# Two walks over sorted edges: a tile-wise ring of 44 instead of two chunk buffers of 20 tiles, and half the descriptor scratch

## The reference

```python
h = (x @ W).reshape(n, heads, out_ch)
al_s = einsum('nhc,hc->nh', h, a_src); al_d = einsum('nhc,hc->nh', h, a_dst)
logits = leaky_relu(al_s[src] + al_d[dst], 0.2)
m = segment_max(logits, dst)                 # per target node
e = exp(logits - m[dst]); denom = segment_sum(e, dst)
out = segment_sum(h[src] * (e / denom[dst]), dst)
```

## Time and profile before

| | us |
|---|---|
| median of 3 runs | 6598.26 |
| lowest and highest | 6596.5 and 6599.07 |
| profiled execution, its own time | 6614.21 |
| profiled execution, span of the core | 6612.5 |
| first walk, in the profile | about 200 to 2850 |
| second walk | about 2850 to 5700 |

### The profile page before, as it was taken

How to read it: one execution, slowest core, us unless ns; L and a number is a source line. 1 busy time by engine, 2 the same in 40 slices (tenths; PEclk the granted TensorE clock), 3 DMA queues, 4 the chain that set the end, 5 groups by cost and what they waited for, 6 DMA issues and landing times. The chain is left out here.

```text
span 6612.5 us, 83222 instructions
## 1 busy us (share of the span) xinstructions
PE 4639.7 (70%) x21069; PEld 3502.2 (53%) x21069; DVE 3115.5 (47%) x8587; ACT 2833.9 (43%) x8419; POOL 3628.4 (55%) x3778
## 2 busy tenths in 40 slices
PE   7477777777777777773556565665555555699999
PEld 4355555555555555552344444444443434588887
DVE  4355656655566656662444444444444444711111
ACT  2455655655556555673434334343232223322222
POOL 0556665665566656535666666666666664234443
PEclk9788898888889888996777777676677777699999
DMA  5667777777777767733444444444455554453332
GB/s 194 191 194 199 203 201 195 200 201 198 197 197 203 202 191 198 197 106 108 117 118 115 119 115 116 120 114 116 117 135 140 138 138 115 155 188 129 128 132 78
DMA packets 703586, 1027.53 MB, mean 155 GB/s; under 512 B 391738, under 2 KB 483736, under 8 KB 702862
## 3 DMA queue, kind: packets, MB, share of 16 engines
q0 software_dynamic: 229312, 718.64, 38.9%
q1 hardware_dynamic: 473246, 302.52, 15.8%
q10 hardware_dynamic: 560, 1.05, 0.1%
HBM read 951.81 MB, written 65.48 MB: 154 GB/s over the span
## 5 line engine op out<-in xcount | busy, mean ns | idle before, releaser
L861 POOL DMA_INDIRECT walk_ring<-s_h,walk_index x3320 | 3167.7, 954 | 2138.2 <-issue 1018.1
L1022 PE MATMUL walk_pM<-walk_ring,walk_hit 128*128 128x262 f32 (+1 forms) x9960 | 3013.1, 454 | 233.6 <-issue 138.8
L1022 PEld LDWEIGHTS walk_pM<-walk_ring,walk_hit 128*128 128x128 f32 x9960 | 2140.1, 224 | 788.1 <-issue 377.3
L886 ACT ACTIVATE walk_ring<-walk_ring 128x128 f32<-128x128 f32 (+1 forms) x6640 | 2138.8, 414 | 19.1 <-issue 13.0
L1252 DVE TENSOR_TENSOR acc<-walk_pM,acc 128x520 f32 (+1 forms) x1494 | 832.5, 557 | 1789.4 <-remote 997.3
L876 ACT ACTIVATE walk_ring<-walk_gap 128x40 f32<-128x40 f32 (+1 forms) x249 | 54.0, 258 | 2582.1 <-DVE walk_gap L1214 2020.0
L926 PE MATMUL walk_pC<-all_ident,walk_best 128*84 128x128 f32 (+1 forms) x166 | 57.4, 346 | 904.5 <-DVE walk_best L1170 639.2
L1219 DVE TENSOR_TENSOR walk_hit<-walk_pK,walk_meta 128x512 f32<-128x512 f32 x830 | 560.2, 675 | 11.8
L926 PEld LDWEIGHTS walk_pC<-all_ident,walk_best 128*84 128x84 f32 (+1 forms) x166 | 19.7, 119 | 970.2 <-issue 970.0
L2061 ACT ACTIVATE expert_hT<-expert_pH,expert_b 128x256 f32<-128x256 f32 x448 | 187.8, 470 | 601.1 <-PE expert_pH L2113 601.0
L2113 PE MATMUL expert_pH<-expert_xT,expert_w 128*128 128x256 f32 x1792 | 398.9, 381 | 6.7 <-DVE expert_xT L2071 5.9
(11 more groups left out here) (314 smaller groups left out, 4245.3 us busy)
## 6 DMA issues: line engine op xcount, KB each, us to landing
walk_hitT<-s_places SPq DMA_DIRECT2D x166, 640.0 KB
expert_w<-in_fw_dram SPq DMA_DIRECT2D x64, 1024.0 KB, 12.0
walk_ring<-s_h,walk_index POOLq DMA_INDIRECT x3320
walk_goal<-walk_target SPq DMA_DIRECT2D x830, 6.0 KB
walk_goal<-walk_target SPq DMA_DIRECT2D x830, 1.5 KB
walk_xk<-s_xT SPq DMA_DIRECT2D x98, 128.0 KB
walk_resets<-s_resets SPq DMA_DIRECT2D x415, 20.0 KB
s_h<-first_h_out SPq DMA_DIRECT2D x7, 1056.0 KB, 4.3
```

Source lines behind the costliest of these rows:

```text
L861: pool.indirect_dma_start(ring[:, r % RS, t, :], None, table, bass.IndirectOffsetOnAxis(ap=index[:, r % TS, t:t + 1], axis=0)).then_inc(ro ...
L886: last = nc.scalar.activation(row, row, ACT.Copy, scale=ring[:, r % RS, t, at + FH:at + FH + 1])
L1022: last = nc.tensor.matmul(pM[:, b, a, 0:WIDE], hit[:, (r * CGROUPS + g) % HBUF, t % GROUP, :], ring[:, r % RS, t, a * HALF_ROW:a * HALF_RO ...
```

## The change

The ring becomes a ring of tiles: `[P, RT, A * HALF_ROW]` with RT = 44 tiles in the first walk (60 in the second, which is the same size as before). Tile t of chunk c lies at slot (c * 20 + t) mod RT. `AHEAD` becomes RT // TPS: 22 steps in the first walk and 30 in the second. Since 44 isn't a multiple of 20, some chunks of the first walk wrap round the end, and every operation on a whole chunk is done there in two pieces. The semaphores `rows_in` become 3 in both walks, the index buffers 5 instead of 6, and `TURN`, after which the written-out phases repeat, 30 instead of 6. Three small tiles share one, and the descriptor scratch is 8192 bytes.

```diff
-TURN = 6
+TURN = 30
...
-    RS = 2 if H > 1 else 3
-    TS = 6
+    RT = 44 if H > 1 else 60
+    TS = 5
...
-    AHEAD = RS * CS
+    AHEAD = RT // TPS
+    RS = 3
+    assert RT % GROUP == 0 and RT >= 2 * CT
...
-        ring = m.sb("ring", [P, RS, CT, A * HALF_ROW])
+        ring = m.sb("ring", [P, RT, A * HALF_ROW])
...
+        small = m.sb("small", [P, 8])
+        carry, reset0, ratio = small[0:RK, 0:2], small[0:1, 2:4], small[0:1, 4:4 + H]
...
+        def slot(c, t):
+
+            return (c * CT + t) % RT
+
+        def pieces(c):
+
+            head = min(CT, RT - slot(c, 0))
+            return [slice(0, head)] + ([slice(head, CT)] if head < CT else [])
...
-                            pool.indirect_dma_start(ring[:, r % RS, t, :], None, table,
+                            pool.indirect_dma_start(ring[:, slot(c, t), :], None, table,
...
                     for a in range(A):
-                        nc.scalar.activation(terms_of(r).rearrange("p (t a) h -> p t a h", a=A)[:, :, a, :],
-                                             gap[:, a * HP:(a + 1) * HP, 1:].rearrange("p h t -> p t h"), ACT.Exp)
+                        for tiles in pieces(n):
+                            nc.scalar.activation(terms_of(n, tiles).rearrange("p (t a) h -> p t a h", a=A)[:, :, a, :],
+                                                 gap[:, a * HP:(a + 1) * HP, 1:].rearrange("p h t -> p t h")[:, tiles, :], ACT.Exp)
...
+                    for tiles in pieces(n):
+                        own = terms_of(n, tiles).rearrange("p (t a) h -> p a h t", a=A)
+                        for a in range(A):
+                            heads = slice(a * HP, (a + 1) * HP)
+                            last = nc.vector.tensor_tensor(best[:, heads, 1 + tiles.start:1 + tiles.stop], own[:, a, :, :],
+                                                           dt[:, tiles, heads].rearrange("p t h -> p h t"), ALU.max)
                     last.then_inc(best_ready, 1)
...
+                    for tiles in pieces(n):
+                        for a in range(A):
+                            nc.vector.tensor_tensor(tail(n, tiles, HP * (FH + 1))[:, :, a, :],
+                                                    peak_h[:, a * HP:(a + 1) * HP, 1:].rearrange("p h t -> p t h")[:, tiles, :],
+                                                    spread(meta[:, r % IS, 1, tiles], 2, HP), ALU.mult)
...
-                        nc.vector.tensor_copy(weight_k, ring[:, r % RS, :, at])
+                        for tiles in pieces(n):
+                            nc.vector.tensor_copy(weight_k[:, tiles], slots_of(n, tiles)[:, :, at])
...
-    nc = bacc.Bacc("TRN2", target_bir_lowering=False, num_devices=1)
+    nc = bacc.Bacc("TRN2", target_bir_lowering=False, num_devices=1, dynamic_dma_scratch_size=8192)
```

More of the change, by code:

```diff
@@ L739, in tables_of, with slots_of, tail, terms_of @@
             return (i * (TURN // IS) + r // IS + 1) * 32
[L741 to L747, removed]
+        def slot(c, t):
[3 more added lines that the diff above has]
+            return [slice(0, head)] + ([slice(head, CT)] if head < CT else [])
+        def slots_of(c, tiles):
+            return ring[:, slot(c, tiles.start):slot(c, tiles.start) + tiles.stop - tiles.start, :]
+        def tail(c, tiles, lo):
+            return slots_of(c, tiles).rearrange("p t (a c) -> p t a c", a=A)[:, :, :, lo:lo + HP]
+        def terms_of(c, tiles):
+            return by_head(slots_of(c, tiles).rearrange("p t c -> p (t c)"), HP, FH)[:, :, :, FH]
         m.clear_semaphores()
@@ L884, in scale @@
                             at = h // HP * HALF_ROW + h % HP * (FH + 1)
-                            row = ring[:, r % RS, t, at:at + FH]
-                            last = nc.scalar.activation(row, row, ACT.Copy, scale=ring[:, r % RS, t, at + FH:at + FH + 1])
+                            row = ring[:, slot(c, t), at:at + FH]
+                            last = nc.scalar.activation(row, row, ACT.Copy, scale=ring[:, slot(c, t), at + FH:at + FH + 1])
                     last.then_inc(act_scaled, 1)
@@ L1022, in multiply @@
                             last = nc.tensor.matmul(pM[:, b, a, 0:WIDE], hit[:, (r * CGROUPS + g) % HBUF, t % GROUP, :],
[L1023 removed]
+                                                    ring[:, slot(c, t), a * HALF_ROW:a * HALF_ROW + WIDE], start=(u == 0), stop=(u == TPS - 1))
                     last.then_inc(multiplied, 1)
@@ L1166, in terms @@
                     dve.wait_ge(rows_in[r % RS], rows_of(i, r))
[L1167 to L1170, removed]
-                    last.then_inc(best_ready, 1)
-                    for a in range(A):
-                        heads, goals = slice(a * HP, (a + 1) * HP), slice(H + a * HP, H + (a + 1) * HP)
-                        nc.vector.tensor_tensor(pair[:, 0, heads, 1:], own[:, a, :, :], dt[:, :, goals].rearrange("p t h -> p h t"), ALU.add)
+                    for tiles in pieces(n):
[4 more added lines that the diff above has]
+                                                           dt[:, tiles, heads].rearrange("p t h -> p h t"), ALU.max)
+                    last.then_inc(best_ready, 1)
+                    for tiles in pieces(n):
+                        own = terms_of(n, tiles).rearrange("p (t a) h -> p a h t", a=A)
+                        for a in range(A):
+                            heads, goals = slice(a * HP, (a + 1) * HP), slice(H + a * HP, H + (a + 1) * HP)
+                            nc.vector.tensor_tensor(pair[:, 0, heads, 1 + tiles.start:1 + tiles.stop], own[:, a, :, :],
+                                                    dt[:, tiles, goals].rearrange("p t h -> p h t"), ALU.add)
                 def scan_tiles(n, i, r):
```

12 lines of the change are left out of this document (4 added, 8 removed).

## The result

| | before | after |
|---|---|---|
| median (4 runs each, same chip) | 6598.66 | 6709.1 |
| lowest and highest | 6596.5 and 6602.86 | 6693.72 and 6716.62 |
| profiled execution, span | 6612.5 | 6714.9 |

The ratio is 1.0157, with a 95% interval of 1.014 to 1.0175. The forecast of 6603 us was wrong, and so was its range, whose upper end was 6632.

What follows compares the result with a forecast made beforehand. The prediction took the first walk as bound by a chain round the engines once per chunk, 31.4 us. Added operations of 14.0 us less 9 for the wait gave +5 us, a median of 6603 us, range 6576 to 6632.

Steps and rivals of the forecast that it cites:

- The gathers don't move against PE: First walk: gathers stay released by PE at the same moments, so traffic within a chunk is unchanged; 0 for new collisions.
- It hides them where it ends by itself: Unnamed wait before the adds covers added `best` and pair operations; half of 9.6 us counted, +4.8 us.
- Its own sign of failure: Forecast wrong if "remote" waits before the adds (286.5 us) change by more than 15 us.
- The wait before `best`, -9 us: DVE's wait for late rows in the first walk nearly goes; half reaches the end, -9 us, bounds 0 and -17.7.
- half of 17.7: Share of DVE's 17.7 us wait for late rows expected to reach the end time, counted as -9 us.
- The rival by which late chunks cost more than their wait: Late rows also slow PE's matmuls, 1.83 us in each of 13 cases; -28 us in all, 6570 us, chance 0.18.
- The added operations, +14 us: Extra DVE and ACT operations in 30 wrapped chunks of the first walk: 14.0 us, bounds 7.2 and 42.
- The rival with each at its full duration, 42 us: Added operations in 30 wrapped chunks cost their whole duration, 42 us, less 9 for the wait: 6631 us, chance 0.20.
- The scratch, 0: The smaller descriptor scratch doesn't hold up POOL's gathers; taken as 0.
- The third rival: Longer ring doesn't bring rows earlier, or small scratch holds POOL; only the added 14 us stay: 6612, chance 0.08.
- estimate of 56 gathers: Descriptor scratch of 8192 bytes, at 16 bytes and 9 descriptors per engine, holds 56 gathers, more than the ring's 44.

Runs made afterwards that it cites:

- e11: Changed kernel with AHEAD 20 instead of 22 in the first walk, on a 6600 chip: 6576.6 us, ratio 0.996.
- e5: The changed kernel run again without edits, on a 6600 chip: 6691.4 us, ratio 1.0135.
- e6: The kernel before, unchanged, on a 6600 chip: 6600.3 us.
- e15: Changed kernel with SP sending the places before the tables and index instead of after, on a 6600 chip: 6575.9 us, ratio 0.9958.
- e7: The changed kernel run again without edits, on a 5690 chip: 5641.9 us, ratio 0.9923.
- e13: Changed kernel with DVE also waiting before `best` for POOL's fourth step of the next chunk, on a 6600 chip: 6688.0 us, ratio 1.0144.
- e4: Changed kernel with a 40-tile first-walk ring, the same 30 chunks still cut in two, on a 5690 chip: 5689.7 us, ratio 0.9985.
- e1: Changed kernel with 40 tiles instead of 44 in the first walk, so nothing wraps, on a 5690 chip: 5682.5 us, ratio 0.9979.
- e3: Kernel before with only the descriptor scratch set to 8192 bytes, on a 5690 chip: 5677.8 us, ratio 0.997.
- e14: Kernel before with one goal transfer of fixed windows per chunk instead of ten, on a 6600 chip: 6469.4 us, ratio 0.9795.
- e12: Changed kernel with one goal transfer of fixed windows per chunk instead of ten, on a 6600 chip: 6458.5 us, ratio 0.9786.
- e2: Changed kernel with AHEAD 20 instead of 22 in the first walk, on a 5690 chip: 5687.0 us, ratio 0.9985.
- e8: Changed kernel with AHEAD 20 instead of 22, run once more on a 5690 chip: 5683.3 us, ratio 0.9994.
- e9: Kernel before with one goal transfer of fixed windows per chunk instead of ten, on a 5690 chip: 5695.0 us, ratio 1.0014.
- e10: Changed kernel with one goal transfer of fixed windows per chunk instead of ten, on a 5690 chip: 5640.5 us, ratio 0.9922.

## Why the prediction was wrong

**The step that failed** is "The gathers don't move against PE. [...] So the traffic at any moment of a chunk stays as it is, and I add nothing for new collisions." In the place of that 0 stood 115 to 130 us (e11 against e5 and the result). The reasoning followed POOL and PE, whose order is indeed tied by `multiplied`, and left out the third party: SP's transfers hang on other events (`added`, `gap_ready`, `spread_out`), and they did move. Worked out from the traces, as means over the chunks of the first walk. The first two rows are in us after the first matmul of the spread, the third is SP's hold before the places as defined above, and the fourth is the period of a chunk:

| | before | after | e6 (before) | e5 (changed) | e11 | e15 | e7 (5690 chip) |
|---|---|---|---|---|---|---|---|
| places transfer issued | 6.01 | 7.24 | 6.38 | 7.06 | 4.81 | 5.97 | 1.12 |
| last goal transfer issued | 18.45 | 19.83 | 18.75 | 19.55 | 18.65 | 21.25 | 11.16 |
| hold before the places | 3.4 | 5.7 | 3.8 | 5.6 | 1.7 | up to 5.1 | 0.05 |
| period | 31.4 | 32.7 | 31.3 | 32.5 | 31.2 | 31.2 | 25.5 |

(In e15 SP's wait for `added` lies within the hold too. The 18.3, 19.7 and 7.05 of the expectations are means over the middle chunks.) The last goal comes 1.38 us later after than before, as much as the period grew (1.35), but that is no rule: from e6 to e5 it is 0.80 us for a period longer by 1.22, and e15 issues its goals later still and is fast. What e15 changes is which transfers stand together and which operation of DVE a hold falls on; that this is why it is fast is argued, not shown.

**The clock as a rival.** The walk's matmuls were busy for 1956.0 us after and 1855.2 before, 101 us more of the 110, and the granted clock was 0.84 for 0.87, further towards its lower level of 1.2 GHz. The other traces of kernels that lose have 0.84 (e5) and 0.85 (e13), e6 and e11 0.87. Against it as the cause: the adds' waits that a matmul ended fell from 330.9 to 228.0 us, and e15 is faster than the kernel before with a clock of 0.86 and matmuls busy for 1888.7 us. That no part of the loss comes by the clock isn't shown.

**Where the profile said so beforehand.** The earlier trace rows had 286.5 us of "remote" before the adds, some thirteen times the wait at the line of the expected gain, and the prediction wrote that it rested on something unexplained. It then counted it as cover that stays where it is ("It hides them where it ends by itself"). It should have been a rival with a price: a cost for which no releaser is known can grow by any change of timing, and the sister rows with the same word (106.3 us at the copy of the ends, 55.9 at the rescaling) were left out of the argument. Its own sign of failure, a change of this wait by more than 15 us, came true: 286.5 became 197.6, while that at the copy of the ends grew by 162.4 (268.7 for 106.3).

**The wait before `best`, -9 us.** The wait went (22.6 to 6.6), and the gain didn't come. In e11 the same wait is 117.0 us in a kernel that is 0.4% faster than before. So on these chips lateness of the rows isn't on the path, and half of 17.7 was still too much. The rival by which late chunks cost more than their wait is refuted by the same run. On the 5690 chips, where POOL is the bound, the wait is real and the change gains 0.8%.

**The added operations, +14 us.** The counts are as worked out: 226 for `best`, `pair`, the tails and the exponentials, and 113 for the copy of the weights. Their price is 7 us by e4 against e1, but on a chip where a wait for rows can hide them. On the 6600 chips it is bounded by the intervals of the wrapped chunks, which grew less than the others, by the 23.5 us that DVE's busy time grew for 210 operations (0.11 us each), and by e11, which has them all and is still faster than before. The rival with each at its full duration, 42 us, finds no support in them. The Trainium skill (VectorE: DVE Perf Modes, The TRN2 errata) has every operation pay its fixed latency; the 0.11 us of busy time for each is less than the 0.157 us that its formula makes at no elements (an estimate, 151 / 0.96 ns), so here the operations overlap in part.

**The scratch, 0.** It holds nothing up: e3 is 0.3% faster than before on its chip, and the gathers stay at 957 ns in the changed kernel for 952. The third rival had the rows no earlier, or POOL held by the scratch; the wait before `best` and these gathers answer both. The prediction's estimate of 56 gathers counts 9 descriptors per engine. In the Trainium skill (DMA: Bandwidth & Descriptors, The descriptor swizzle) there are 9 for reading and another 9 for writing, in a plain transfer of 1 MiB. So 56 holds only if the two sides don't share a partition's scratch, which no run here shows.

**How the transfers bind the engines.** Shown is that ten goal transfers in the place of one cost 134 us in the kernel before (e14) and 233 to 251 in the changed one (e12 against e5 and the result, on other chips), on 6600 chips alone, and that there engines wait although what they depend on is done: 627.6 us of DVE's idle time in the first walk after has "remote" as its releaser, 496.8 before, 400.1 in e11 and none in e7. Not shown is that SP's transfers are what holds them. The Trainium skill (DMA: Bandwidth & Descriptors, Issuing engines are not separate DMA queues) has transfers of every engine run on the same 16 DMA engines and interleave. No row here shows the interleaving itself: the 10.77 us are the issue of ten transfers, and the same ten are issued in 6.4 us in e7. Bandwidth isn't what is short, since the share of the DMA engines is 0.68 after and 0.84 in the faster first walk of e7.

**What stays open.** What holds DVE, POOL and SP in the "remote" waits, and what part SP's transfers have in it; how two steps of gathers come to lengthen these waits (the two runs meant for it missed); why the changed kernel with AHEAD 20 is 0.4% faster than before on a 6600 chip; and whether it is the chip or a condition of it that separates the 6600 from the 5690 ones. As for versions: on a 6600 chip e15 (6575.9 us) and e11 (6576.6) beat both kernels. e11's edit brings nothing on a 5690 chip (e2, e8), and e15 wasn't run on one, so e15 is the one to try next.

## What to carry to other kernels

Ask of a longer ring not only whether its wait is on the path, but which other queue's transfers will now fall on which operation. Idle time without a recorded releaser that is many times larger than the gain is a term of the range and not cover: list it by line, put the ends of these waits beside the transfers over all chunks, since a single one can look like a rule (19 of 66 here), and ask what they hang on. And run the kernel before beside every candidate on the same chip, since one change can be a gain of 0.8% on one and a loss of 1.6% on another.

## What the runs showed of the hardware

- The same kernel takes 6600 us on three chips and 5690 on three others, 14% less, and on none of those used here a time between the two. On the faster ones the first walk has no "remote" wait at the lines above. In e3, the kernel before with half the scratch, the copy of the ends waits 0.9 us for 118.2, and the adds 259.3 for 690.3:

```profile
L1252 DVE TENSOR_TENSOR acc<-walk_pM,acc 128x520 f32 x747 | 520.1, 696 | 259.3 <-PE walk_pM L1022 241.7 <-DVE acc L1252 17.6
L1185 DVE COPY walk_pC<-walk_row_ahead 1x4 f32<-1x4 f32 x83 | 12.0, 144 | 0.9 <-PE walk_pC L932 0.9
```

- Small transfers issued by SP can cost time on engines that don't wait for them. Ten transfers of one chunk's goals took 10.77 us to issue beside the gathers. One in their place gave the kernel before 2.1% (e14) and the changed one 3.5 to 3.7% (e12 against e5 and the result) on 6600 chips, and nothing on a 5690 chip (e9, e10).
- On the 6600 chips a wait can end microseconds after what it waits for is done, also for SP itself: its places transfer comes 3.4 us late on average in the kernel before, 5.7 in the changed one, 1.7 in that with AHEAD 20, and 0.05 on a 5690 chip (e7).
- POOL issues an indirect DMA of 128 rows every 1.25 us where it doesn't wait, and 20 of them take 25.0 us of a chunk of 25.5 us on a 5690 chip (e7).
